# Bulk loads of the first stage issued by GpSimd, behind its first constants, in place of by ScalarE

## The chip, the cores and the metric

The kernel runs on one core of a Trainium2 chip. The metric is the device time of one execution in microseconds, the median of several runs. The core has five engines with instruction streams of their own: TensorE (PE; its weight loads are shown as PEld), VectorE (DVE), ScalarE (ACT), GpSimd (POOL) and SyncE (SP). They order their work by semaphores. Any of SyncE, ScalarE and GpSimd can issue a DMA, as an instruction in its own stream; the transfer then runs on the core's 16 DMA engines.

## The reference, cut to what matters

The whole program is a graph network with two layers over 1250 nodes of 512 features and 40,000 edges, each layer followed by a mixture of experts:

```python
x = x + _L0_gnn_ref(_layernorm(x), edge_attr_4, edge_attr_8, edge_index, W_up0, W_up1, W_mlp1..4, W_out0, W_out1)
x = x + _L0_ffn_ref(_layernorm(x)[None], ...)[0]      # routed experts
x = x + _L1_gnn_ref(_layernorm(x), edge_index, ...)   # graph attention, two rounds
x = x + _L1_ffn_ref(_layernorm(x)[None], ...)[0]      # routed experts
```

The change touches the first stage of the first line alone. That stage computes three things that depend little on each other:

```python
# 1. path-weight MLP of every edge: 8 -> 64 -> 64 -> 64
h = edge_feats
for W in (W_mlp1, W_mlp2, W_mlp3):
    h = SILU_2MOM * silu(h @ W / sqrt(W.shape[0]))
# 2. the node rows: layer norm of x, then products with W_up0 and W_up1
x0, x1 = _lin_irreps(node_feats[:, :128], node_feats[:, 128:].reshape(n, 128, 3), W_up0, W_up1)
# 3. tables of the sorted receivers (dst) and of the senders (src), for the stage that follows
```

## The kernel before, in words

The program calls six stages one after the other: `prepare`, `edges`, `update`, `routed_experts`, `graph_layers`, `last_layers`. `prepare` (lines 117 to 475) and `edges` are each one block: every engine has its own program in it, and the next block begins when all engines have ended theirs.

**Tiling of `prepare`.** The 40,000 edges are 80 groups of 500. The MLP works on pairs of groups stacked on the 128 partitions, four pairs at a time: ten iterations (`ITER = 10`, `B = 4`). In an iteration TensorE does a first layer (line 364), a second and a third (line 374) on four PSUM banks, and ScalarE answers each bank with a Silu (line 426), so there are 12 Silus of 128x500 in an iteration. The input of the first layer is `ea`, in four buffers, loaded by SyncE (line 207); its weights are `w1q`, `w2h` and `w3h`, loaded by SyncE too (lines 210, 211 and 215; `w1q` after GpSimd has cleared it, line 241). The third layer's result goes to DRAM (`hidden`, line 225, SyncE).

**Node rows.** The ten 125-row tiles of `x` are loaded into `xs` (the tile called `z` in the profile). VectorE takes their statistics as they land (lines 276 and 279). From iteration `LEAD = 4` on, ScalarE takes one square root for all ten tiles (line 459, on the semaphore `stats_ok`), VectorE applies the norm (line 287), TensorE transposes and multiplies two tiles in each iteration (lines 382, 384 and 392, with the weights `wu`), ScalarE copies (lines 432 and 438) and GpSimd writes the rows to `node_table` in DRAM (line 265).

**Tables.** VectorE reduces `dst` (`dsts`, line 291), later works on `dst_rows` and `src_rows` (line 312 on, after a wait on `all_in`, 16 for each of five loads, and on `ids`, 7 operations of GpSimd), and waits at line 327 for a table that SyncE has written and read back through DRAM. ScalarE scales `w4` in iteration 7 (line 455), after `all_in` too.

**ScalarE's stream** begins with 12 DMA issues, lines 443 to 451: five for `x` (500 KB each), one for `dst`, two for `w_up0` and `w_up1`, one each for the receivers' rows, the senders' rows and the edge attributes `y`, two for `w_mlp4`. Then come the ten iterations. **GpSimd's stream** begins with the clearing of `w1q`, the identity matrix (lines 60 and 63) and `eps` (line 243), then the triangular matrix `before` (lines 245 and 247), five iotas, the clearing of the two accumulators `macc` and `cacc` (lines 259 and 260), a wait on `ids`, and the ten writes to `node_table`, each after a wait on `us_ok`.

In `edges` GpSimd gathers rows of `node_table` (line 565), SyncE loads `hidden` (line 555), and the three compute engines work on them.

Of the kernel before, what the change touches and what calls it, by code (L numbers as in the profile page):

```python
# [17 lines left out]
P = 125  # L18
T = N // P
# [3 lines left out]
EG = C * P  # L23
G = E // EG
MUL = 128
HID = 64
# [31 lines left out]
def identity(nc, pool, ticks, ident):  # L58

    ticks(nc.gpsimd.memset(ident, 0.0))  # L60
    ticks.wait()
    size = ident.shape[1]
    return ticks(nc.gpsimd.affine_select(out=ident, in_=ident, compare_op=ALU.not_equal, fill=1.0, base=0,
                                         pattern=[[-1, size]], channel_multiplier=1))
# [47 lines left out]
def prepare(nc, queue, tables, xs, xn, spare, src, dst_p, ea4, w_mlp4, x, dst, ea8, w_up0, w_up1, w_mlp, node_table, hidden, steps, bases):  # L112
# [7 lines left out]
    with ctx:  # L120
        def sb(name, shape, dt=F32):
            return ctx.enter_context(nc.sbuf_tensor("p1_" + name, shape, dt))
# [4 lines left out]
        def sem(name):  # L127
            return nc.alloc_semaphore("p1_" + name)
# [7 lines left out]
        wu = sb("wu", [128, 2, 128])  # L136
# [9 lines left out]
        dsts = sb("dst", [G, EG], I32)  # L146
# [18 lines left out]
        x_in = [sem(f"x_in{k}") for k in range(T // 2)]  # L165
        dst_in = sem("dst_in")
        w_in = sem("w_in")
        up_in = sem("up_in")
# [16 lines left out]
        all_in = sem("all_in")  # L185
# [10 lines left out]
        def tiles_after(i):  # L196

            return [2 * (i - LEAD), 2 * (i - LEAD) + 1] if LEAD <= i < LEAD + T // 2 else []

        with nc.Block() as block:  # L200
# [37 lines left out]
            @block.gpsimd  # L238
            def _(pool):
                pool_ticks = Ticks(pool, consts)  # L240
                nc.gpsimd.memset(w1q[:], 0.0).then_inc(wz, 1)
                identity(nc, pool, pool_ticks, ident[:])
                pool_ticks(nc.gpsimd.memset(eps[:], EPS))

                pool_ticks(nc.gpsimd.memset(before[:], 1.0))
                pool_ticks.wait()
                pool_ticks(nc.gpsimd.affine_select(out=before[:], in_=before[:], compare_op=ALU.is_gt, fill=0.0,
                                                   base=0, pattern=[[1, G]], channel_multiplier=-1))

                nc.gpsimd.iota(tables.columns[:], [[1, WIN]], base=0, channel_multiplier=0,  # L250
                               allow_small_or_imprecise_dtypes=True).then_inc(ids, 1)
                nc.gpsimd.iota(tables.spots[:], [[1, 4 * WIN]], base=0, channel_multiplier=0,
                               allow_small_or_imprecise_dtypes=True).then_inc(ids, 1)
                nc.gpsimd.iota(tables.row_id[:], [[0, 1]], base=0, channel_multiplier=1).then_inc(ids, 1)
                nc.gpsimd.iota(tables.node_ids[:], [[1, CS]], base=-1, channel_multiplier=0,
                               allow_small_or_imprecise_dtypes=True).then_inc(ids, 1)
                nc.gpsimd.iota(tables.blocks[:], [[1, WINS]], base=0, channel_multiplier=0,
                               allow_small_or_imprecise_dtypes=True).then_inc(ids, 1)
                nc.gpsimd.memset(tables.macc[:], 0.0).then_inc(ids, 1)
                nc.gpsimd.memset(tables.cacc[:], 0.0).then_inc(ids, 1)  # L260
                pool.wait_ge(ids, 7)

                for t in range(T):
                    pool.wait_ge(us_ok, t + 1)
                    pool.dma_start(node_table[t * P:(t + 1) * P, :], us[:, t % 2, :]).then_inc(us_out[t % 2], 16)
                for b in range(2):
                    pool.wait_ge(us_out[b], 16 * (T // 2))
# [151 lines left out]
            @block.scalar  # L419
            def _(act):  # L420
                def silu(i, h, ps_ok, h_ok, scale):
                    for b in range(B):
                        act.wait_ge(ps_ok, i * B + b + 1)
                        if h is h3 and i:
                            act.wait_ge(h3_out[b], 16 * i)
                        nc.scalar.activation(h[:, b, :], psH[b][:], ACT.Silu, scale=scale).then_inc(h_ok, 1)

                def turned(t):
                    act.wait_ge(xt_mm, t + 1)
                    if t >= 2:  # L430
                        act.wait_ge(us_mm, t - 1)
                    nc.scalar.activation(xt[:, t % 2, :, :], psT[:], ACT.Copy).then_inc(xt_ok, 1)

                def node_rows(t):
                    act.wait_ge(us_mm, t + 1)
                    if t >= 2:
                        act.wait_ge(us_out[t % 2], 16 * (t // 2))
                    nc.scalar.activation(us[:, t % 2, :], psU[0:P, :, :].rearrange("p j n -> p (j n)"), ACT.Copy,
                                         scale=float(MUL) ** -0.5).then_inc(us_ok, 1)

                rows = x.rearrange("(t p) d -> p t d", p=P)
                for k in range(T // 2):
                    act.dma_start(xs[:, 2 * k:2 * k + 2, :], rows[:, 2 * k:2 * k + 2, :]).then_inc(x_in[k], 16)
                act.dma_start(dsts[:], dst.rearrange("(g e) -> g e", e=EG)).then_inc(dst_in, 16)
                act.dma_start(wu[:, 0, :], w_up0).then_inc(up_in, 16)
                act.dma_start(wu[:, 1, :], w_up1).then_inc(up_in, 16)
                act.dma_start(tables.dst_rows[:].rearrange("p g c -> p (g c)"), dst_p).then_inc(all_in, 16)
                act.dma_start(tables.src_rows[:].rearrange("p g c -> p (g c)"), src).then_inc(all_in, 16)
                act.dma_start(tables.y[:].rearrange("p g c m -> p (g c m)"), ea4).then_inc(all_in, 16)
                for half in range(2):  # L450
                    act.dma_start(tables.w4[half * HID:(half + 1) * HID, :], w_mlp4).then_inc(all_in, 16)
                for i in range(ITER):
                    if i == LEAD + 3:
                        act.wait_ge(all_in, 16 * 5)
                        nc.scalar.activation(tables.w4[:], tables.w4[:], ACT.Copy, scale=SILU_GAIN / 8.0)
                    if i == LEAD:
                        act.wait_ge(stats_ok, 1)
                        act.wait_ge(consts, 3)
                        nc.scalar.activation(std[:], mv[:, :, 1], ACT.Sqrt, bias=eps[:]).then_inc(std_ok, 1)
                    tiles = tiles_after(i)  # L460
                    silu(i, h1, mm1, h1_ok, 8.0 ** -0.5)
                    if tiles:
                        turned(tiles[0])
                    silu(i, h2, mm2, h2_ok, SILU_GAIN / 8.0)
                    if tiles:
                        node_rows(tiles[0])
                        turned(tiles[1])
                    silu(i, h3, mm3, h3_ok, SILU_GAIN / 8.0)
                    if tiles:
                        node_rows(tiles[1])  # L470
# [2250 lines left out]
```

## Time and profile before

| | |
|---|---|
| Time before, median of 3 runs | 2344.52 us (2343.66 to 2349.13) |
| The profiled execution's own time | 2353.07 us |
| Span of the profiled execution | 2351.4 us |
| Mean granted TensorE clock | 0.917 |
| ScalarE busy | 1118.3 us (48%) |
| GpSimd busy | 748.9 us (32%) |
| Bytes that ScalarE's DMA queue (q10) moved | 4.07 MB |

The profile is of one execution; its times count from the start of the span. Engines' names with a q (ACTq, SPq) are the sequencers that issue DMAs; an issue has a start and a duration in the profile but is not counted as busy time. The landing of a DMA is when its semaphore has come up. The granted clock is a share of TensorE's full clock of 2.4 GHz; it has two levels, 1.00 and 0.50.

### The profile page before, as it was taken

The numbers are of one execution on the slowest core, as the hardware profiler recorded it, in microseconds if no ns is written. First come the engines' busy times: TensorE is split into PE (matmuls) and PEld (weight loads), VectorE is DVE, ScalarE is ACT, GpSimd is POOL, SyncE is SP. The second block draws the span as 40 slices with busy tenths as digits, with TensorE's granted clock in tenths as the row PEclk, the third lists the DMA queues.
The fourth block names the chain that finished last, engine by engine and source line by source line (L and its number), as shares of the span: only waits on it lengthen the run. The fifth ranks groups of instructions, "written<-read, shape, count | busy, mean of one in ns | idle before, by whom it ended". The sixth has DMA issues, their size and how long they took to land. (4 is left out here: it accounts for less than half of the span.)

```text
span 2351.4 us, 36494 instructions
## 1 busy us (share of the span) xinstructions
PE 2003.0 (85%) x11260; PEld 1288.4 (55%) x11261; DVE 1513.0 (64%) x2331; ACT 1118.3 (48%) x2278; POOL 748.9 (32%) x629
## 2 busy tenths in 40 slices
PE   5899999999997738999975497999999999980997
PEld 2444444444445727777732444777344777540997
DVE  1289999999995774333348865777763778428011
ACT  5777777777773404555510313666001676210332
POOL 4287777777770012444453000000000000000453
PEclk9989999999998957999988598999999999995998
DMA  5565555555551423788544313000012100221794
GB/s 160 168 170 157 154 155 154 153 154 152 155 155 53 95 85 129 268 261 265 174 129 132 96 43 115 22 22 1 18 43 81 64 22 1 104 100 46 221 277 94
DMA packets 200741, 285.12 MB, mean 121 GB/s; under 512 B 116698, under 2 KB 128677, under 8 KB 196543
## 3 DMA queue, kind: packets, MB, share of 16 engines
q0 software_dynamic: 98272, 142.08, 21.2%
q1 hardware_dynamic: 100158, 137.67, 19.0%
q10 hardware_dynamic: 2209, 4.07, 0.5%
q8 instruction: 56, 0.92, 0.2%
q14 instruction: 46, 0.38, 0.0%
HBM read 233.52 MB, written 49.84 MB: 121 GB/s over the span
## 5 line engine op out<-in xcount | busy, mean ns | idle before, releaser
L565 POOL DMA_INDIRECT p_s<-node_table,e_src_rows x320 | 454.5, 1420 | 147.4 <-issue 86.7
L2004 PE MATMUL g_psO<-g_h,g_ring 125*125 125x257 f32 x1600 | 372.4, 388 | 19.7 <-DVE g_ring L2136 10.3
L2004 PEld LDWEIGHTS g_psO<-g_h,g_ring 125*125 125x125 f32 x1600 | 296.6, 190 | 92.1 <-DVE g_stage L2130 26.6
L703 PE MATMUL p_psW<-e_w,p_hid 64*125 64x512 f32 x640 | 275.4, 654 | 50.2 <-ACT z L580 24.7
L622 DVE TENSOR_TENSOR g_b<-z,p_s 125x1536 f32<-125x1536 f32 x160 | 273.6, 1751 | 0.0
L711 PE MATMUL p_psM<-g_b 125*32 125x384 f32 x648 | 249.5, 533 | 11.0 <-DVE p_key L684 5.9
L580 ACT ACTIVATE z<-p_psW 125x512 f32<-125x512 f32 x320 | 187.2, 585 | 147.0 <-PE p_psW L703 139.0
L715 PE MATMUL p_psM<-g_b 125*32 125x256 f32 x648 | 218.8, 422 | 0.0
L714 PE MATMUL p_psM<-g_b 125*32 125x256 f32 x648 | 211.3, 410 | 0.0
L713 PE MATMUL p_psM<-g_b 125*32 125x256 f32 x648 | 193.8, 426 | 0.0
L585 ACT ACTIVATE p_of<-e_node_ids,z 125x314 bf16<-125x314 f16 x320 | 176.2, 551 | 6.8 <-PE p_psC L720 3.1
L2069 ACT ACTIVATE g_ring<-g_ring,g_ident 125x625 f32<-125x625 f32 x160 | 131.0, 819 | 85.3 <-DVE g_ring L2117 84.5
L703 PEld LDWEIGHTS p_psW<-e_w,p_hid 64*125 64x125 f32 x640 | 71.6, 185 | 181.2 <-ACT z L580 113.8
L2136 DVE SCALAR_TENSOR_TENSOR g_ring<-g_ring,g_cnt 125x625 f32<-125x625 f32 x160 | 128.7, 804 | 39.2 <-ACT g_ring L2069 39.1
L1954 PE MATMUL g_psO<-g_a,g_b 128*125 128x512 f32 x320 | 141.2, 603 | 2.1 <-PEq L1907 2.1
L2093 DVE CUSTOM_DVE_ANT_0 g_ring<-g_rb,g_far 125x1250 f32<-125x1250 f32 x80 | 110.7, 1453 | 49.7 <-DMA g_rb<-sender_rows 49.7
L60 POOL MEMSET p_ident<- 128x128 f32 x5 | 1.0, 206 | 434.2 <-POOLq L2669 368.1
L1438 PE MATMUL p_ps<-p_xt,p_first_own 128*128 128x128 f32 x1120 | 138.4, 277 | 0.0
L1399 POOL DMA_INDIRECT p_xg<-z_rows,p_node_at x70 | 71.1, 1016 | 210.8 <-DVE p_y L1535 154.4
L712 PE MATMUL p_psM<-g_b 125*32 125x128 f32 x648 | 135.9, 294 | 0.0
L1438 PEld LDWEIGHTS p_ps<-p_xt,p_first_own 128*128 128x128 f32 x1120 | 132.6, 194 | 0.5 <-issue 0.5
L1450 PE MATMUL p_ps<-p_second_own,p_ht 128*128 128x512 f32 x280 | 131.6, 593 | 0.0
(357 smaller groups left out, 3775.2 us busy)
## 6 DMA issues: line engine op xcount, KB each, us to landing
p_ring<-in_L_ffn_weights SPq DMA_DIRECT2D x32, 1025.0 KB
slot_rows<-p_y POOLq DMA_DIRECT2D x70, 256.0 KB
p_w1s<-in_L_ffn_w SPq DMA_DIRECT2D x16, 1024.0 KB
g_a<-in_L_ffn_w SPq DMA_DIRECT2D x16, 1024.0 KB
hidden<-g_b SPq DMA_DIRECT2D x40, 250.0 KB, 3.2
p_hid<-hidden SPq DMA_DIRECT2D x160, 62.5 KB
g_rb<-receiver_rows SPq DMA_DIRECT2D x16, 610.4 KB
p_s<-node_table,e_src_rows POOLq DMA_INDIRECT x320
```

The source lines that it names most:

```text
L565: pool.indirect_dma_start(s[:, g % 4, c, :, :].rearrange("p k u -> p (k u)"), None, node_table, bass.IndirectOffsetOnAxis(ap=src_rows[:, g ...
L580: nc.scalar.activation(w[:, b, c, :, :].rearrange("p k u -> p (k u)"), psW[c % 2][0:P, :], ACT.Copy).then_inc(w_ok, 1)
L585: nc.scalar.activation(of[:, b, c, :], node_ids[:], ACT.Sigmoid, scale=STEEP, bias=rise[:, bass.ds(g, 1), c:c + 1].rearrange("p o c -> p ( ...
L622: last = nc.vector.tensor_tensor(msg[:, b, :, q:q + 3, :], w[:, b, :, p:p + 1, :].broadcast_to([P, C, 3, MUL]), s[:, at, :, 1:4, :], ALU.mult)
L703: nc.tensor.matmul(psW[c % 2][0:P, :], hid[part, b, c // 2, :], w4[part, :], start=True, stop=True)\
L711: nc.tensor.matmul(psM[i][0:32, 0:3 * MUL], a, rows_[:, 0:3, :], start=begin, stop=end)
L713: nc.tensor.matmul(psM[i][64:96, 0:2 * MUL], own[1], rows_[:, 4:7:2, :], start=begin, stop=end)
L714: nc.tensor.matmul(psM[i][32:64, MUL:3 * MUL], own[0], rows_[:, 4:6, :], start=False, stop=end)
L715: last = nc.tensor.matmul(psM[i][96:128, 0:2 * MUL], own[2], rows_[:, 4:8:3, :], start=begin, stop=end)
L1438: last = nc.tensor.matmul(psH[u % 2][:, m * 128:(m + 1) * 128], w1s[u % 2][:, k, m * 128:(m + 1) * 128], xt[:, u % 2, k, :], start=k == 0, ...
L1954: last = nc.tensor.matmul(psO[0:P, 2 * (t % 2) + j, :], xt[:, k, t * P:(t + 1) * P], ws[:, k, j * 512:(j + 1) * 512], start=k == 0, stop=k ...
L2004: last = nc.tensor.matmul(psO[0:P, j, 0:HW], ring[:, i % RING, j * P:(j + 1) * P], h[:, s, hd, :], start=s == 0, stop=s == T - 1)
```

## The change

The 12 DMA issues leave ScalarE's stream and stand, in the same order and with the same semaphores, in GpSimd's stream, behind the memset of `eps` and ahead of the memset of `before`. Nothing else differs.

```diff
                 identity(nc, pool, pool_ticks, ident[:])
                 pool_ticks(nc.gpsimd.memset(eps[:], EPS))
+                rows = x.rearrange("(t p) d -> p t d", p=P)
+                for k in range(T // 2):
+                    pool.dma_start(xs[:, 2 * k:2 * k + 2, :], rows[:, 2 * k:2 * k + 2, :]).then_inc(x_in[k], 16)
+                pool.dma_start(dsts[:], dst.rearrange("(g e) -> g e", e=EG)).then_inc(dst_in, 16)
+                pool.dma_start(wu[:, 0, :], w_up0).then_inc(up_in, 16)
+                pool.dma_start(wu[:, 1, :], w_up1).then_inc(up_in, 16)
+                pool.dma_start(tables.dst_rows[:].rearrange("p g c -> p (g c)"), dst_p).then_inc(all_in, 16)
+                pool.dma_start(tables.src_rows[:].rearrange("p g c -> p (g c)"), src).then_inc(all_in, 16)
+                pool.dma_start(tables.y[:].rearrange("p g c m -> p (g c m)"), ea4).then_inc(all_in, 16)
+                for half in range(2):
+                    pool.dma_start(tables.w4[half * HID:(half + 1) * HID, :], w_mlp4).then_inc(all_in, 16)
 
                 pool_ticks(nc.gpsimd.memset(before[:], 1.0))
...
-                rows = x.rearrange("(t p) d -> p t d", p=P)
-                for k in range(T // 2):
-                    act.dma_start(xs[:, 2 * k:2 * k + 2, :], rows[:, 2 * k:2 * k + 2, :]).then_inc(x_in[k], 16)
-                act.dma_start(dsts[:], dst.rearrange("(g e) -> g e", e=EG)).then_inc(dst_in, 16)
-                ... (the same eight lines, with act in place of pool)
                 for i in range(ITER):
```

## Rows read from the trace of the kernel before

**Rows 1.** The page, chain that ended last: the shares by engine.
```profile
PE 10%; DVE 2%; POOL 0%; DMA 0%; issue 0%; ACT 0%; POOLq 0%
```

**Rows 2.** Timeline of ScalarE, 0 to 35 us: start, duration, operation, count, idle before.
```profile
0.82 10.92 ACTq L443 DMA_DIRECT2D z<-in_x  x5
...
25.09 1.28 ACT L426 ACT_TABLE_LOAD   x1 [24.94 <-issue]
26.39 2.02 ACT L426 ACTIVATE p_h<-p_psH 128x500 f32<-128x500 f32 x4
```

**Rows 3.** Timeline of TensorE, 8 to 35 us.
```profile
12.38 2.05 PE L364 MATMUL p_psH<-p_ea,p_w1q 16*128 16x500 f32 x8 [12.38 <-DMA p_ea<-in_edge_attr]
27.03 4.08 PE L374 MATMUL p_psH<-p_h,p_w2h 64*64 64x500 f32 x16 [12.60 <-ACT p_h L426]
```

**Rows 4.** Timeline of ScalarE, 38 to 56 us.
```profile
40.64 2.02 ACT L426 ACTIVATE p_h<-p_psH 128x500 f32<-128x500 f32 x4 [0.26 <-PE p_psH L364]
...
46.77 2.02 ACT L426 ACTIVATE p_h<-p_psH 128x500 f32<-128x500 f32 x4 [0.26 <-PE p_psH L364]
...
52.66 1.28 ACT L459 ACT_TABLE_LOAD   x1
```

**Rows 5.** Timeline across the stage's end: ScalarE, SyncE, then TensorE.
```profile
101.79 3.98 ACT L426 ACTIVATE g_b<-p_psH 128x500 f32<-128x500 f32 x8
...
109.32 2.53 SPq L555 DMA_DIRECT2D p_hid<-hidden  x4
...
112.28 2.07 PE L703 MATMUL p_psW<-e_w,p_hid 64*125 64x512 f32 x4 [7.32 <-DMA p_hid<-hidden]
```

**Rows 6.** Timeline of SyncE, two stretches near 7 us.
```profile
3.40 2.90 SPq L215 DMA_DIRECT2D p_w1q<-in_L_gnn_W_mlp  x8
...
7.17 1.34 SPq L207 DMA_DIRECT2D p_ea<-in_edge_attr  x3
```

**Rows 7.** The first row is the landings of `ea` from 0 to 30 us, then `bases`.
```profile
DMA to landing us min/median/max: 2.2/3.4/5.3
...
DMA to landing us min/median/max: 7.6/7.6/7.6
```

**Rows 8.** All on line 2561: a table load, and ScalarE's idle time before it.
```profile
L2561 ACT ACT_TABLE_LOAD x1 | 1.3, 1283 | 13.4 <-DVE p_mv L2363 13.4
```

**Rows 9.** Stretches: length, busy of PE, PEld, DVE, ACT, POOL, clock, DMA share, GB/s.
```profile
22.00:24.00 2.00, 0.00 (x0) 0.00 (x0) 1.29 (x2) 0.00 (x0) 2.00 (x1) 1.00 0.32 123
53.00:55.00 2.00, 0.80 (x3) 0.00 (x0) 0.67 (x2) 1.97 (x3) 0.00 (x0) 1.00 1.01 352
56.00:59.00 3.00, 2.79 (x14) 1.41 (x16) 3.00 (x8) 2.89 (x7) 0.00 (x0) 0.50 0.04 11
110.00:160.00 50.00, 42.38 (x224) 18.51 (x224) 34.96 (x41) 32.47 (x72) 40.67 (x31) 0.76 0.61 167
```

**Rows 10.** The page, DMA queues: packets, MB, share; q10 is ScalarE's.
```profile
q10 hardware_dynamic: 2209, 4.07, 0.5%
```

**Rows 11.** Timeline of GpSimd, 0 to 70 us.
```profile
1.65 0.09 POOL L243 MEMSET p_eps<- 125x1 f32 x1
...
16.14 10.82 POOL L260 MEMSET e_cacc<- 128x12874 uint16 x1
62.17 0.80 POOL L265 DMA_DIRECT2D node_table<-p_us  x1 [35.21 <-ACT p_us L438]
```

**Rows 12.** GpSimd's DMA issues elsewhere, by line: durations in ns, or busy us and mean.
```profile
L265 POOL DMA_DIRECT2D node_table<-p_us x10: 532/532/801, 62.2 to 99.8; - x10
...
L565 POOL DMA_INDIRECT p_s<-node_table,e_src_rows x320 | 454.5, 1420 | 147.4 <-issue 86.7 <-DVE g_b L622 60.8
```

**Rows 13.** Timeline of VectorE, 0 to 93 us.
```profile
26.83 1.29 DVE L276 BATCH_NORM_STATS2 p_stats<-z 125x6 f32<-125x512 f32 x2 [3.20 <-DMA z<-in_x]
...
64.94 0.33 DVE L312 CAST p_sender<-e_src_rows 125x320 f32<-125x320 int32 x1
...
92.08 0.48 DVE L353 TENSOR_TENSOR z<-z,p_window_of 125x320 f32<-125x320 f32 x1
```

More of the change, by code:

```diff
@@ L439, in node_rows @@
                                          scale=float(MUL) ** -0.5).then_inc(us_ok, 1)
-                rows = x.rearrange("(t p) d -> p t d", p=P)
-                for k in range(T // 2):
-                    act.dma_start(xs[:, 2 * k:2 * k + 2, :], rows[:, 2 * k:2 * k + 2, :]).then_inc(x_in[k], 16)
-                act.dma_start(dsts[:], dst.rearrange("(g e) -> g e", e=EG)).then_inc(dst_in, 16)
[L445 to L451, printed above, removed]
                 for i in range(ITER):
```

## The prediction

> **What bounds the kernel now.** I read the chain of waits first, to see whether it reaches the place of the change. It doesn't: its shares add up to some 12% of the span, counted back from the end, and the first stage lies over 90% before it [rows 1]. So the first stage has to be read by itself: what sets its end, and does the rest follow its end one for one? For that I took the timeline of each engine, one after the other, up to 125 us.
>
> ScalarE's timeline: from 0.82 to 25.09 us it does nothing but issue the 12 bulk loads; the idle time before its first table load is 24.94 us, released by "issue", that is, by nothing but its own instructions. The first Silu starts at 26.39 [rows 2]. TensorE's timeline: the first layer's products are started at 12.38, when the last `ea` load has landed, and their four groups end at 14.43. Then TensorE waits 12.60 us for ScalarE [rows 3]. So the MLP's input is there long before ScalarE is.
>
> Afterwards ScalarE is the pacer: an iteration takes 46.77 - 40.64 = 6.13 us, with 0.26 us of idle time in it [rows 4]. The last Silus start at 101.79 and end at 105.77; SyncE stores them, the block ends, and SyncE's first load of the next stage is issued at 109.32 [rows 5]. Every engine's work of the later stages stands behind that block's end. Whatever the first Silu gains, and no other wait takes, the end of the span gains.
>
> **The change part by part.**
>
> *Removed: 12 issues from ScalarE.* Its stream can then reach the wait for the first product right away. What is late next is that product. It starts at 12.38 [rows 3]; what it waits for is issued by SyncE, not by ScalarE, and SyncE's order is untouched: eight small loads from 3.40 to 6.30, then `ea`, whose fourth issue starts when the third, at 7.17, has ended, about 7.6 us [rows 6]. I keep 12.38.
>
> From the first product to the first Silu: the four groups take 2.05 us, a group about half of that, and with its latency some 1.1 us, an estimate from the 2.05 us of the row [rows 3]. A table load of 1.28 us follows [rows 2]. Does it come ahead of the wait or behind it? Line 2561 shows one that started only when a wait for VectorE of 13.4 us was over [rows 8]. So I put it behind: first Silu at 12.38 + 1.1 + 1.28 + 0.1 = 14.9 us. Gain: 26.39 - 14.9 = 11.5 us. If it comes ahead of the wait, the gain is 12.8.
>
> Bounds of the first product, which the trace of before does not show under the new traffic: its fourth `ea` load could land as fast as the quickest, 2.2 us after 7.6, at 9.8; the eight `w1q` loads end their issue at 6.30 and are then no later than that. Or it could take as long as the slowest small transfer of the stage, 7.6 us (`bases`), and land at 15.2 [rows 6, 7]. That is -2.6 and +2.8 us about 12.38, so a gain between 8.7 and 14.1, with the table load ahead of the wait 15.4. I take no shift, as the row of before (4.8 us for this load) lies between, and it had the same 4.07 MB in flight beside it [rows 10].
>
> *Added: 12 issues to GpSimd, between `eps` and `before`.* `eps` ends at 1.74 us [rows 11]. A plain issue of 125 rows costs GpSimd 0.53 us, an indirect one of 125 rows 1.42 us [rows 12]. The `x` loads have 250 row pieces each, so 1.06 us each, 5.3 us; `dst` (80 rows) 0.4; the two `wu` (128 rows) 1.1; the two row tables 1.1; `y` 0.5; the two halves of `w4` (64 rows) 0.6: about 9 us. By the indirect rate it would be 24 us, about what ScalarE needs for them now, 24.3 us [rows 2]. I take 9, as these are plain issues, and keep 24 as the other end.
>
> Behind them on GpSimd stand 26.96 - 1.74 = 25.2 us of constants, mostly two memsets [rows 11]. They would end at 36 us, at the long end at 51. Who waits? TensorE's wait for the identity is met before the loads. VectorE waits for the iotas at line 312, at 64.94, in the new time 53.4 [rows 13]. The first write of `node_table` is due at 62.17, in the new time 50.7 [rows 11]. So at 9 us of issuing there are 14 us of slack and the cost is nothing; at 24 us the first write is 0.5 us late, and its buffer is wanted again only an iteration later. VectorE's tables end at 92.56, 13 us ahead of the last Silu [rows 5, 13]. Cost between 0 and 0.5 us; I take 0.
>
> *Moved: the start of the loads.* The first `x` issue goes from 0.82 to 1.74 us. The last statistics start at 26.83 now [rows 13], and ScalarE wants them at 52.66 [rows 4], in the new time 41.2. So `x` may land 14 us later than now before it costs anything. `dst`, `wu` and the tables are wanted later still. Cost 0.
>
> A rule that bears on this: in the stretch in which nearly only these loads run, the DMA share is 0.32, five engines out of sixteen, at 123 GB/s [rows 9]. The Trainium skill, "DMA: Bandwidth & Descriptors", section "Why a DMA increments its semaphore by 16 and not by 1", says that a DMA issued by ScalarE uses the largest number up to 16 that divides the row count (5 for 125 rows), while one from GpSimd may use all 16. The row agrees for ScalarE; no row here shows a 125-row load from GpSimd. By it the loads end sooner, which nothing waits for, but lie on all the engines at the time when `ea` is fetched.
>
> *Sum.* 11.5 us off the profiled execution's 2353.07 gives 2341.6. That execution is 8.6 us above the median of 2344.52; the median less 11.5 is **2333.0 us**.
>
> **The rivals.**
>
> *A. GpSimd's queue starves SyncE's loads (slower).* GpSimd writes its requests faster than they are carried out, so that nearly 4 MB stand in the queue when SyncE asks for `ea` at 6.3. If `ea` had to wait for all of it, the first product comes when the 4.07 MB are through. At 167 GB/s, the rate of the stretch with GpSimd's gathers [rows 9, 10], that is 24.4 us from about 2.9, so 27.3; the first Silu is at 29.8 and the time 3.4 us longer: 2347.9. It decides from a first product after 23.9 us. For it: the loads would no longer leave eleven DMA engines free. Against it: in that same stretch of gathers SyncE's loads get through, and at 352 GB/s, which the DMA engines reach at 53 us [rows 9], all is through at 14.5, a first Silu at 17.0 and a gain of 9.4, which is in the forecast. Chance 0.06.
>
> *B. GpSimd becomes the late one.* Its issues take long because the queue is full and each waits for room, as ScalarE's x issues do now (10.92 us for five) [rows 2]. It costs nothing up to 24 us. At 30 us the constants end at 57, the first write of `node_table` is 6 us late and takes a part of the gain, up to 6: 2333 to 2339. Chance 0.06.
>
> *C. It is hidden anyway.* ScalarE's early start only makes it wait elsewhere, for instance at the square root for `x`, and the stage ends as before: 2344.5. Against it: the 14 us of slack above. The same page of the Trainium skill, "Issuing engines are not separate DMA queues", says that issuing from several engines saves only issue time, which is "usually small relative to the DMA itself". Here the trace disagrees about the size, with 24.3 us of issuing and 12.60 us of waiting for it [rows 2, 3]. Chance 0.05.
>
> *D. Given back later.* The stage ends early, but TensorE's clock falls at other places. In this stage it was at 0.50 from 56 to 59 us, and in the 50 us after the stage's end it is 0.76 in the mean [rows 9]. A quarter of these 50 us is lost to the low level; a drift of a third of that, 4 us, would leave a gain of 7.5 and, with a late `ea`, less than can be told: 2337 to 2341. Chance 0.11.
>
> **How the numbers follow.** Forecast 0.72, A 0.06, B 0.06, C 0.05, D 0.11. A measurement of this kernel can tell a difference of about 0.3%, 7.0 us. The forecast's own range, a gain from 8.7 to 15.4, is 2329.1 to 2335.8, and clears 7.0 us. B clears it about half the time, D about a third. A is slower by more than 7.0 us only where the queue is slower than its 167 GB/s, half of its chance. So faster 0.78, within 0.3% 0.19, slower 0.03. For the range I add D and B at the upper side, and leave out A and C: 2329 to 2340.
>
> **What would show it.** The first Silu of ScalarE near 14.9 us instead of 26.39, with TensorE's first product near 12.4; GpSimd's constants ended near 36 us; the last Silu near 94.3 and SyncE's first load of the next stage near 97.8. The square root must not wait for the statistics. The prediction is wrong if the first product moves beyond 19 us, if GpSimd's issues take over 27 us, or if the next stage begins 11 us earlier and the span doesn't end so.

## The result, and the profile after

The changed kernel takes 2338.78 us in the median of 20 runs, the kernel before 2343.25 us in 20 runs beside them. The ratio is 0.9978, with a 95% interval of 0.9970 to 0.9985: 3.5 to 7.0 us faster, 5.2 at the middle. 2333.0 us with a range of 2329 to 2340 was forecast. The time lies in the range, but the gain is less than half of the 11.5 us in the sum. The profiled execution of before was a long one, 2353.07 us. Its second stage, from SyncE's first load of it (109.32) to SyncE's first DMA of the stage behind it (740.63), took 631.3 us; in the profile of after it takes 620.7 us, in those of the ten experiments 620.5 to 622.0, three of which are made from the kernel before. So 10.6 of the 14.9 us between the two spans (2351.4 and 2336.5 us) are not the change's, and what follows is read within the first stage.

The moved issues are thirteen, not the twelve that the text so far counts: five for `x`, one for `dst`, two for `wu`, one each for the two row tables and `y`, two for `w4`. The prediction's sum of 9 us has a price for each of the thirteen.

ScalarE's timeline after, from 0 to 35 us; it answers to [rows 2]:

```profile
0.82 1.28 ACT L437 ACT_TABLE_LOAD   x1 [0.67 <-PEq L2712]
21.23 2.02 ACT L437 ACTIVATE p_h<-p_psH 128x500 f32<-128x500 f32 x4 [19.12 <-PE p_psH L375]
```

The issues are gone and the table load has moved to the very start. But the first Silu comes at 21.23 and not at 14.9: ScalarE waits 19.12 us for TensorE. TensorE's timeline, which answers to [rows 3]:

```profile
19.19 2.05 PE L375 MATMUL p_psH<-p_ea,p_w1q 16*128 16x500 f32 x8 [19.19 <-DMA p_ea<-in_edge_attr]
```

SyncE's, in two stretches, which answers to [rows 5, 6]:

```profile
3.37 4.35 SPq L215 DMA_DIRECT2D p_w1q<-in_L_gnn_W_mlp  x8
7.76 15.40 SPq L207 DMA_DIRECT2D p_ea<-in_edge_attr  x20
...
104.94 1.24 SPq L555 DMA_DIRECT2D p_hid<-hidden  x2
```

The first product has slipped from 12.38 to 19.19, and it waits for `ea`. The gain of the first Silu is 26.39 - 21.23 = 5.16 us, that of the next stage's first load 109.32 - 104.94 = 4.38 us. Both lie within the interval of the measured gain.

The first product needs the fourth `ea` load. In the kernel before it is issued at 7.62, in this one it has this row:

```profile
10.36 0.63 SPq L207 DMA_DIRECT2D p_ea<-in_edge_attr  x1
```

So the 6.81 us have two parts. SyncE issues that load 2.74 us later, since its own issues take longer: the eight of `w1q` 4.35 us in place of 2.90, the second and third of `ea` 1.07 and 1.08 us in place of 0.42 and 0.41. And from its issue to the product it takes 8.83 us in place of 4.76, which is 4.07 us more.

The longer landing stands first in the landings of the DMAs up to 30 us; compare [rows 7]. The last number of a row is the median from issue to landing; the last row has `ea` alone:

```profile
z<-in_x POOLq DMA_DIRECT2D x5, 500.0 KB, 11.9
p_ea<-in_edge_attr SPq DMA_DIRECT2D x20, 31.2 KB, 8.5
...
DMA to landing us min/median/max: 5.7/8.5/10.2
```

And in two stretches of 2 us, with the columns of [rows 9]:

```profile
12.00:14.00 2.00, 0.00 (x0) 0.00 (x0) 0.15 (x1) 0.00 (x0) 1.93 (x10) 1.00 1.05 196
16.00:18.00 2.00, 0.00 (x0) 0.00 (x0) 0.98 (x2) 0.00 (x0) 2.00 (x1) 1.00 1.00 193
```

The DMA engines are all busy (share 1.00 to 1.05; between 10 and 20 us the mean is 1.05, and was 0.71 in the kernel before), and move only 193 to 196 GB/s. `ea` takes 8.5 us to land in place of 3.4, in the median. GpSimd's side went nearly as forecast: it issues for 10.4 us (9 in the sum), and its constants end at 37.85 (36 in the forecast). Its timeline answers to [rows 11]:

```profile
2.13 6.05 POOL L246 DMA_DIRECT2D z<-in_x  x5 [0.39 <-issue]
...
11.47 1.08 POOL L254 DMA_DIRECT2D e_w<-in_L_gnn_W_mlp  x2
...
27.03 10.82 POOL L271 MEMSET e_cacc<- 128x12874 uint16 x1
57.38 0.58 POOL L276 DMA_DIRECT2D node_table<-p_us  x1 [19.53 <-ACT p_us L449]
```

### The profile page after: what moved, and what is told of

It is laid out like the page before. It is cut to its first block and busy times, and to the rows that moved or that the text cites. A ratio compares the mean times of both kernels' runs of the same rounds, so it can differ in the third digit from the quotient of the medians.

```text
span 2336.5 us, 36494 instructions
## 1 busy us (share of the span) xinstructions
PE 1995.6 (85%) x11260; PEld 1282.3 (55%) x11261; DVE 1510.5 (65%) x2331; ACT 1119.9 (48%) x2278; POOL 803.1 (34%) x642
## 2 busy tenths in 40 slices
DMA packets 201059, 285.12 MB, mean 122 GB/s; under 512 B 118164, under 2 KB 129559, under 8 KB 196862
## 5 line engine op out<-in xcount | busy, mean ns | idle before, releaser
L565 POOL DMA_INDIRECT p_s<-node_table,e_src_rows x320 | 496.7, 1552 | 107.7 <-issue 107.7
L2004 PE MATMUL g_psO<-g_h,g_ring 125*125 125x257 f32 x1600 | 372.4, 388 | 19.7 <-DVE g_ring L2136 10.3
L711 PE MATMUL p_psM<-g_b 125*32 125x384 f32 x648 | 242.2, 520 | 17.2 <-DVE g_b L622 7.7
L715 PE MATMUL p_psM<-g_b 125*32 125x256 f32 x648 | 213.7, 413 | 0.0
L714 PE MATMUL p_psM<-g_b 125*32 125x256 f32 x648 | 205.9, 401 | 0.0
L713 PE MATMUL p_psM<-g_b 125*32 125x256 f32 x648 | 187.5, 415 | 0.0
```

Source lines behind the costliest of these rows:

```text
L565: pool.indirect_dma_start(s[:, g % 4, c, :, :].rearrange("p k u -> p (k u)"), None, node_table, bass.IndirectOffsetOnAxis(ap=src_rows[:, g ...
L711: nc.tensor.matmul(psM[i][0:32, 0:3 * MUL], a, rows_[:, 0:3, :], start=begin, stop=end)
L713: nc.tensor.matmul(psM[i][64:96, 0:2 * MUL], own[1], rows_[:, 4:7:2, :], start=begin, stop=end)
L714: nc.tensor.matmul(psM[i][32:64, MUL:3 * MUL], own[0], rows_[:, 4:6, :], start=False, stop=end)
L715: last = nc.tensor.matmul(psM[i][96:128, 0:2 * MUL], own[2], rows_[:, 4:8:3, :], start=begin, stop=end)
L2004: last = nc.tensor.matmul(psO[0:P, j, 0:HW], ring[:, i % RING, j * P:(j + 1) * P], h[:, s, hd, :], start=s == 0, stop=s == T - 1)
```

## The experiments

The twelve kernels in one table: start of TensorE's first product, of ScalarE's first Silu and of SyncE's first load of the next stage, in us, and the ratio to the kernel before.

| kernel | product | Silu | next stage | ratio (95%) |
|---|---|---|---|---|
| before | 12.38 | 26.39 | 109.32 | 1 |
| after | 19.19 | 21.23 | 104.94 | 0.9978 (0.9970 to 0.9985) |
| loads behind the product | 9.53 | 11.56 | 106.53 | 0.9975 (0.9963 to 0.9986) |
| one load at a time | 11.91 | 13.95 | 131.03 | 1.0073 (1.0051 to 1.0096) |
| ScalarE, 112 and 13 rows | 15.05 | 17.09 | 100.37 | 0.9954 (0.9938 to 0.9971) |
| behind the product, shared | 6.63 | 8.70 | 102.31 | 0.9959 (0.9943 to 0.9975) |
| hardware queues early | 8.63 | 10.70 | 97.12 | 0.9957 (0.9933 to 0.9981) |
| memsets beside the norm | 12.88 | 27.39 | 132.70 | 1.0070 (1.0052 to 1.0089) |
| GpSimd, 112 and 13 rows | 14.23 | 16.26 | 98.08 | 0.9944 (0.9926 to 0.9961) |
| small loads late | 19.35 | 21.39 | 104.50 | 0.9975 (0.9960 to 0.9989) |
| GpSimd, ten loads by tile | 14.38 | 16.41 | 99.52 | 0.9942 (0.9927 to 0.9956) |
| best | 10.82 | 12.88 | 98.14 | 0.9931 (0.9919 to 0.9943) |

**Loads behind the first product** (after, with one wait in GpSimd's stream):

```diff
+                pool.wait_ge(mm1, 1)
                 rows = x.rearrange("(t p) d -> p t d", p=P)
```

> The changed kernel with one wait more: GpSimd issues the 12 bulk loads only when the first product is done (mm1 at 1). Theory S (the bulk loads, backlogged on GpSimd's queue, lie on all 16 DMA engines ahead of SyncE's ea loads): with no bulk traffic the first product comes at 9.5 to 10.5 us instead of 19.19, the first Silu 2.0 us later at 12, 9 us ahead of the changed kernel; x lands by 32, before the square root wants it at 38.5; time 2343.3 - 14 = 2329, ratio to before 0.994. Rival C (what delays the ea loads is not the bulk traffic, for instance SyncE's own issues): first product stays at 17 to 19, ratio 0.998. Rival G (the span does not follow the stage's end): first Silu at 12 but ratio still 0.997 to 0.999.

The first half came as the theory says: product at 9.53. The gain did not. ScalarE's waits up to 60 us (sum, times, longest):

```profile
ACT g_b L438 <- DMA hidden<-g_b: 7.5, 4, 3.6
```

A stretch behind them:

```profile
30.00:34.00 4.00, 3.86 (x6) 0.82 (x4) 2.02 (x13) 1.39 (x3) 4.00 (x1) 0.50 1.01 262
```

The bulk loads now met SyncE's stores of `hidden`. ScalarE may not overwrite `h3` before these are through and waited 7.5 us. TensorE starved (from 24 to 30 us it was busy for 2.79 us), and then its clock was at 0.50 from 30 to 40 us. The first Silu is 9.67 us ahead of the changed kernel's, the next stage begins 1.59 us behind it. This is none of the theories in full: bulk traffic is what delays, but pushing it back moves the delay to the next small transfers.

**One load at a time** (after, with a wait for each landing):

```diff
                     pool.dma_start(xs[:, 2 * k:2 * k + 2, :], ...).then_inc(x_in[k], 16)
+                    pool.wait_ge(x_in[k], 16)
```

> The changed kernel, but GpSimd waits for each x load to land before it issues the next thing. The number of DMA engines used is the same, the backlog is at most one load. If it is the backlog that delays ea, the landing of ea falls from 8.5 to 3 or 4 us in the median and the first product comes at 12 to 14. If one load on all 16 engines is enough, it stays at 17 to 19. Each x load takes 3 to 4 us from issue to landing then, so GpSimd's constants end near 50 instead of 37.9, still free or nearly (node rows are first written at 57.4 in the changed kernel, 51 here). Time 2343.3 - 10 = 2333 by the backlog, 2338 otherwise.

The backlog is the cause: the median landing of `ea` fell to 2.6 us and the product to 11.91. The cost was misjudged twice. Alone, an `x` load still takes 8.6 to 10.1 us to land, where 3 to 4 were expected. And the loads and constants now run so late that this row appears (VectorE's norm; smallest, median, largest in ns):

```profile
L299 DVE TENSOR_SCALAR g_b<-z,p_mv,p_rstd x10: 527/542/24989, 52.3 to 81.1; 125x512 f32<-125x512 f32 x10
```

**ScalarE with cut rows** (before, with each `x` load in two, and the wait in `x_in` doubled):

```diff
-                    act.dma_start(xs[:, 2 * k:2 * k + 2, :], ...).then_inc(x_in[k], 16)
+                    for lo, hi in ((0, 112), (112, P)):
+                        act.dma_start(xs[lo:hi, 2 * k:2 * k + 2, :], ...).then_inc(x_in[k], 16)
```

> The kernel before, with ScalarE still the issuer, but each x load cut in two by rows, 112 and 13 in place of 125, so that it may use more DMA engines (the DMA share should rise from 0.32 toward 0.9 while they run). Theory S says: with the loads on all engines ea lands later than before, first product at 15 to 19 instead of 12.38, although GpSimd issues nothing; ScalarE's issuing gets shorter, to 12 to 18 us instead of 24.3, so the first Silu is at about 18 to 21 and the time 2343.3 - 6 = 2337. If it is GpSimd's queue that matters and not the spread, the first product stays at 12 to 13 and the first Silu comes as soon as ScalarE has issued, at 15 to 20.

ScalarE's timeline, TensorE's, and a stretch (its last two columns are DMA share and GB/s):

```profile
0.82 5.16 ACTq L444 DMA_DIRECT2D z<-in_x  x10
```

```profile
15.05 2.05 PE L364 MATMUL p_psH<-p_ea,p_w1q 16*128 16x500 f32 x8 [15.05 <-DMA p_ea<-in_edge_attr]
```

```profile
5.00:10.00 5.00, 0.00 (x0) 0.00 (x0) 2.86 (x5) 0.00 (x0) 5.00 (x1) 1.00 1.08 272
```

The spread alone, with GpSimd's queue out of play, delays the product by 2.7 us. It also takes the issuing from 24.3 to 11.1 us. The DMA share is 1.08 where it was 0.32 [rows 9]. So the issue time is not a fixed price of thirteen DMAs: eighteen take less than half of it. That it hangs on how fast the DMA engines take the transfers fits these rows; nothing here measures it by itself. The kernel before gains 3 to 6 parts in a thousand by that cut, without the change, and that is at least what the change gives (1.5 to 3.0).

**Behind the product, with the first loads shared out** (the first run, with ScalarE issuing the first four `ea` loads, `w2h` and `w3h`):

> As the run with the bulk loads behind the first product, and the loads that the first product needs are shared out: ScalarE, idle at the start, issues the four ea loads of the first iteration and then w2h and w3h; SyncE begins with w1q. SyncE's eight w1q issues end at 3.3, ScalarE's eight at about 5, landing 2.2 later: first product at 7 to 7.5 instead of about 10, first Silu at 9.2, gain on before 17 us, time 2326, ratio 0.993. If the landing of small loads and not their issue sets the product, it comes at 8.5 or later and the gain over the first run is under 1.5.

The product came at 6.63, earlier than expected, but the next stage only at 102.31; the stores of `hidden` took 7.1 us of ScalarE's time again. The ratio's interval overlaps with that of the first run.

**Hardware queues early** (before, with the first loads shared out as in the last run, the `x` loads, cut, from SyncE behind `w1q`, and the eight small ones from GpSimd at 16 us):

> The kernel before, with the early loads on the two hardware queues: ScalarE issues the four ea loads of iteration 0, w2h and w3h; SyncE issues w1q, then the x loads cut 112 and 13 rows, then the other ea loads; the seven small ones (dst, wu, tables, w4) are issued by GpSimd between its two long memsets, at 16 us. If what took the gains back was GpSimd's queue with its long backlog, the hidden stores (from 16 us on) find a nearly empty queue: first product at 7 to 8.5 us, first Silu at 9 to 10.5, no wait of ScalarE for a hidden store over 0.5 us, SyncE's first load of the next stage at 92.5 to 94.5 (109.32 before), time 2344 - 16 = 2328, ratio 0.993. If bulk traffic costs its time wherever it runs, the next stage begins at 98 or later, ratio 0.996.

Between the two: waits for `hidden` of 1.6 us, the next stage at 97.12. The stores meet the tail of the other loads here too, so it isn't GpSimd's queue alone.

**Memsets beside the norm** (before, with one wait):

```diff
+                pool.wait_ge(std_ok, 1)
                 nc.gpsimd.memset(tables.macc[:], 0.0).then_inc(ids, 1)
```

> The kernel before, with one wait: GpSimd starts its two long memsets (13.2 and 10.8 us) only when ScalarE has taken the square root, so that they run beside VectorE's norm of line 287. Theory L (VectorE's op of that line cannot start or end while GpSimd's memsets hold the memory port, as the 24,989 ns instance in the run with one load at a time suggests): one instance of line 287 takes about 24 us in place of 0.46, TensorE's first transpose comes 24 us late, the time is 20 to 25 us longer, ratio 1.009 to 1.011. Rival M (the 25 us there came from late DMA traffic): line 287 keeps 0.46 us in each instance; only the node_table writes are 16 us late, which costs 5 to 8 us, ratio 1.002 to 1.004.

The timelines of GpSimd, VectorE (its first two norms) and TensorE:

```profile
54.69 13.22 POOL L260 MEMSET e_macc<- 128x15744 f32 x1 [51.66 <-ACT p_std L460]
```

```profile
54.92 13.27 DVE L288 TENSOR_SCALAR g_b<-z,p_mv,p_rstd 125x512 f32<-125x512 f32 x1
```

```profile
68.11 11.12 DVE L288 TENSOR_SCALAR g_b<-z,p_mv,p_rstd 125x512 f32<-125x512 f32 x1
```

```profile
68.33 0.44 PE L383 MATMUL p_psT<-p_ident,g_b 125*128 125x125 f32 x1 [14.16 <-DVE g_b L288]
```

VectorE's operation of half a microsecond ends 0.3 us after the memset that began 0.2 us before it. The next one takes 11.12 us and ends 0.3 us after the second memset (67.84 to 78.95), the third again 0.53. So theory L had the total right, 24 us, and not its form, one instance of 24. In the run with one load at a time the slow instance lies from 55.72 to 80.71 and the two memsets from 56.45 to 80.43, so the same explains it. It is the cliff that the change moved toward: its constants now end at 37.85, the norm begins at 49.6. Not every VectorE instruction stops: the statistics take their 1.29 us for two beside a memset of the kernel before too, from 22 to 24 us [rows 9].

The Trainium skill, "SBUF — State Buffer", section "Who interferes with whom", says that VectorE in a two-port mode and GpSimd contend for one pair of ports, which whoever is first holds for its whole instruction. The rows agree in the length of the wait; the port itself no run shows.

The next stage begins 23.4 us later and the ratio says 16.4 us (12 to 21). The first Silu was 1.00 us later already (27.39), ahead of anything that the edit touches; the rest of the difference I did not follow.

**GpSimd with cut rows** (after, with the same cut as ScalarE's):

> The changed kernel with GpSimd's x loads cut into 112 and 13 rows. If the slow landing of x there (8.3 us for a single one) came from an uneven spread of 125 rows over the DMA engines, the 448 KB parts land in about 4.5 us as from ScalarE, x is in by 16 instead of 22.9 and the first product comes at 15 to 16 instead of 19.19, ratio 0.996. If it is GpSimd's way of issuing, x is in at 22 to 25, first product at 18 to 20, and ten issues in place of five make GpSimd's constants 2 to 3 us later, which costs nothing: ratio 0.998.

The landing of its larger `x` loads, and GpSimd's queue over the span (packets, MB, share):

```profile
z<-in_x POOLq DMA_DIRECT2D x5, 448.0 KB, 6.1
```

```profile
q0 software_dynamic: 99520, 146.16, 22.7%
```

The larger `x` loads land in 6.1 us in place of 11.9, the product comes at 14.23, a little earlier than expected, and the gain more than doubles. The queue carries the same bytes in 1280 packets fewer than in the changed kernel, whose row is:

```profile
q0 software_dynamic: 100800, 146.17, 22.6%
```

The changed kernel has 118,164 packets under 512 bytes and this one 116,884, again 1280 fewer: the five loads carry 256 small packets each beside their data.

**Small loads late** (after, with the eight small ones between the memsets):

> The changed kernel with only the five x loads in front; the seven small ones (1.5 of 4.07 MB) are issued between the two long memsets. They stand behind x in the queue in the changed kernel, so if only what lies in front of ea in GpSimd's queue delays it, the first product stays near 19 us and the time the same, ratio 0.998. If the DMA engines' total load at that time matters, they no longer share it: first product at 15 to 17, x in by 20, ratio 0.996 to 0.997.

Product at 19.35, the time the same: what stands behind `x` in the queue costs `ea` nothing.

**Ten loads by tile** (after, with `x` cut by tile and the wait doubled; every load has 125 rows):

```diff
-                    pool.dma_start(xs[:, 2 * k:2 * k + 2, :], ...).then_inc(x_in[k], 16)
+                    for t in (2 * k, 2 * k + 1):
+                        pool.dma_start(xs[:, t:t + 1, :], rows[:, t:t + 1, :]).then_inc(x_in[k], 16)
```

> The control to the run with rows cut 112 and 13: ten x loads from GpSimd here too, but cut by tile, each of 125 rows. Theory R (a load of 125 rows from GpSimd is broken into many small packets: 416 for 0.51 MB, against 160 when cut 112 and 13): the packets of GpSimd's queue stay above 2500, the first product stays at 18 to 21 us, ratio 0.997 to 0.999. Rival N (two smaller DMAs in place of one, whatever their rows, are what made it fast): first product at 14 to 15, ratio 0.994 to 0.995.

GpSimd's queue, and TensorE's timeline:

```profile
q0 software_dynamic: 99520, 146.16, 22.7%
```

```profile
14.38 2.05 PE L376 MATMUL p_psH<-p_ea,p_w1q 16*128 16x500 f32 x8 [14.38 <-DMA p_ea<-in_edge_attr]
```

My theory of the 125 rows fell. Loads of 125 rows and one piece a row are as good as those of 112 and 13 rows with two; of the three shapes run, only 125 rows and two pieces a row in one DMA has the small packets. Rival N named the time rightly; whether any smaller DMA would do, as it says, was not tried. Size alone is a weak reason: 448 KB are nearly the 500 KB, and have neither the packets nor the delay. That the small packets cause the delay is argued from both going together, and why that shape is broken up stays open.

SyncE's timeline splits what the shape costs. The fourth `ea` load is issued at 7.59 in the run with cut rows, at 7.62 in this one and at 7.67 in ScalarE's with cut rows, all as in the kernel before (7.62). It is late only beside the uncut loads issued back to back: 10.36 in the changed kernel, 10.70 with the small loads late. From there to the product it takes 6.64, 6.76 and 7.38 us in the three with cut loads, 8.83 and 8.65 in the other two, 4.76 before. So the spread bulk loads cost `ea` 1.9 to 2.6 us of landing, from whichever engine they are issued, and the uncut shape from GpSimd adds about 2 us of landing and the 2.7 us of late issue. Why SyncE's issues are slow beside it stays open: the mean DMA share was 0.42 from 4 to 6 us and 0.67 from 6 to 8 in the changed kernel, less than the 0.89 and 1.01 in the run with cut rows.

**Best** (after, with the cut rows, the shared first loads, and the small ones late):

> The changed kernel with what the runs so far point to: GpSimd's x loads cut 112 and 13; ScalarE issues the first ea loads, w2h and w3h while it is idle; SyncE begins with w1q; GpSimd issues wu, dst and the row tables between its two memsets and y and w4 behind them. First product at 7.5 to 9, first Silu at 9.5 to 11, waits of ScalarE for hidden stores under 1.5 us in all, SyncE's first load of the next stage at 93 to 96 (109.32 before), time 2345 - 16 = 2329, ratio 0.993. If bulk traffic and the first iterations' small transfers still meet, it stays at 97 to 98, ratio 0.995, the same as with the rows cut alone.

TensorE's timeline, and a stretch (the clock is the third column from the end):

```profile
10.82 2.05 PE L373 MATMUL p_psH<-p_ea,p_w1q 16*128 16x500 f32 x8 [10.82 <-DMA p_w3h<-in_L_gnn_W_mlp]
```

```profile
36.00:38.00 2.00, 2.00 (x16) 0.74 (x12) 0.00 (x0) 1.30 (x3) 2.00 (x4) 0.50 0.31 71
```

The ratio is the expected 0.993, but the stage missed its marks: the product came at 10.82 (7.5 to 9 expected), the next stage at 98.14 (93 to 96), though ScalarE waited for `hidden` only 0.4 us. 2330.44 us in the median, the fastest, and 0.9953 of the changed kernel (0.9931 / 0.9978, two comparisons with the kernel before). The first Silu is 3.4 us ahead of that of the run with cut rows, but the next stage begins at the same time, 98.1. About 2.6 us went before the square root, and the clock was at 0.50 from 36 to 38 us; that run had 1.00 there. Why the clock fell was not tested.

## Why the prediction was right or wrong

- *ScalarE's issues bound the stage.* Right: without them the first Silu starts 2.04 us after the first product.
- *"I keep 12.38".* This is the step that failed. The product came at 19.19, 6.81 us later, beyond my bound of 15.2 and even beyond the 19 that I had called a sign of being wrong. Of that, 2.74 us are SyncE's issues, which I had put at their old times because their order is untouched, and 4.07 us the landing. The late issues, and half of the longer landing, came only beside the uncut loads from GpSimd. The reason that I gave for no shift, "it had the same 4.07 MB in flight beside it", is wrong: in the kernel before, ScalarE had issued only the five `x` loads by 11.77, and spent until 25.09 on all; GpSimd had issued everything by 12.55. The bound took the slowest small transfer of a stretch in which the DMA engines had no such backlog. Rival A had the mechanism, bulk loads in front of `ea`, but at its full price of 24.4 us and a chance of 0.06. Of the 14.9 us by which it would shift the product, under half came true. The runs give the parts: with the loads held back the product is at 9.53; loads spread over the engines, from ScalarE, put it at 15.05; from GpSimd, in an even shape, at 14.2 to 14.4; the shape with the small packets takes it to 19.19.
- *Table load behind the wait.* Wrong; the alternative of 12.8 us had it right. It ran at 0.82, before the wait, and 1.28 us of the sum were not owed; but from product to Silu it took 2.04 us, not 1.1. Together: 11.5 - 6.81 + 0.44 = 5.1 us, the 5.16 of the row.
- *The issues cost GpSimd 9 us and nobody waits.* Right: 2.13 to 12.55, 10.4 us. The cover of 12 us before the norm is real but has a cliff of 24 us behind it, which I had not priced: I asked who waits for the constants' semaphores, not whom the memsets block.
- *The stage's gain is the span's.* Right for the change: 4.38 us against 5.2 (3.5 to 7.0). Of the ten experiments six lie within their intervals too, for instance 8.95 against 10.8 (6.8 to 14.5) and 11.24 against 13.1 (9.1 to 17.4). Four don't: "loads behind the product" 2.79 against 5.9 (3.3 to 8.7), "ten loads by tile" 9.80 against 13.6 (10.3 to 17.1), "best" 11.18 against 16.2 (13.4 to 19.0), and "memsets beside the norm", a loss of 23.4 against 16.4 (12.2 to 20.9). In all four the ratio is kinder than the stage. One profile of each kernel stands behind the stage's figures, and the same one of before behind all; what made the difference stays open.
- *The rivals.* Rival C is refuted by the interval of the ratio, which leaves out 1; rival B by the 10.4 us. In the stage 0.8 us were lost between the first Silu and the end. Rival D would have had the clock give the gain back. It didn't: in the 50 us behind the stage's end the granted clock is 0.82 (third number from the end), and was 0.76 in the kernel before [rows 9]. In the experiments that starved TensorE it did fall.

```profile
105.00:155.00 50.00, 44.20 (x273) 19.47 (x273) 39.19 (x48) 36.34 (x81) 40.65 (x29) 0.82 0.60 156
```

- *The time in the range is luck.* The forecast's own range ended at 2335.8 us, a gain of 8.7, and the measured 2338.78 and 5.2 lie outside it. They lie inside 2329 to 2340 because the upper side was widened for rivals B and D, and neither happened. The measured difference is one within 0.3%, which I had given 0.19.

## What to carry to other kernels

Before bulk loads are moved to another queue, look at what small transfers are on the way at that time, and who waits for them; the issue time saved can be paid again in their landing. When an engine seems to spend long on issuing, look at the DMA share of that stretch: at 0.32 it was the transfers' shape, and cutting it helped whichever engine issued. A long memset on GpSimd is free only while VectorE has nothing to do that it blocks, such as the norm here.

## What the runs showed of the hardware that was not expected

- A GpSimd load of 125 rows with two 2 KB pieces a row carries 256 packets under 512 bytes beside its data, and lands in 11.9 us in the median, 8.6 to 10.1 alone; in two DMAs, 5.5 to 6.1 us.
- ScalarE's thirteen issues took 24.3 us with 125-row loads and 11.1 with the `x` loads cut in 112 and 13 rows, though that makes them eighteen.
- Beside such uncut loads, issued back to back by GpSimd, SyncE's own issues take longer: eight for `w1q` 4.35 us. They took 2.90 to 2.93 beside the cut ones, though the DMA engines were busier there.
- VectorE's 0.5 us norm took 13.27 us beside GpSimd's memset of 13.22, and 24.99 us beside two.
